# Negating the row maxima of two heads with one VectorE instruction in a graph attention kernel

## The reference: what is computed

```python
q, k, v = (proj(Wq, bq), proj(Wk, bk), proj(Wv, bv))
scores = jnp.einsum('bhqd,bhkd->bhqk', q, k) * SCALE
scores = scores * (adj_matrix + bond_matrix)[:, None, :, :]   # both are adj
attn = jax.nn.softmax(scores, axis=-1)
ctx = jnp.einsum('bhqk,bhkd->bhqd', attn, v)
out = jnp.einsum('bse,fe->bsf', ctx, Wo) + bo
return _layernorm(x + out)
```

## Time and profile before

| | us |
|---|---|
| median of 3 runs (437.01 to 439.08) | 437.6 |
| the profiled execution | 432.45 |
| its span in the trace | 430.8 |
| DVE busy | 387.9 (90%), 1592 instructions |
| PE busy | 383.4 (89%) |
| ACT busy | 360.5 (84%) |
| POOL busy | 249.6 (58%) |

### The profile page before, as it was taken

One profiled execution on the slowest core, in us unless ns is written; L12 is line 12 of the kernel. 1 busy time (PEld: TensorE's weight loads), 2 busy tenths in 40 slices (PEclk: granted clock), 3 DMA queues, 4 the chain that ended last, 5 costly groups with the idle time before them and its releaser, 6 DMA issues.

```text
span 430.8 us, 12136 instructions
## 1 busy us (share of the span) xinstructions
PE 383.4 (89%) x3628; PEld 291.0 (68%) x3628; DVE 387.9 (90%) x1592; ACT 360.5 (84%) x1223; POOL 249.6 (58%) x379
## 2 busy tenths in 40 slices
PE   8968999998989899998999999899898999997682
PEld 6755767776767676675777667677766767775452
DVE  4687999999999999999899999989999999999965
ACT  4588899888888888888988888899888789988760
POOL 3330656748385664748567474856747385554455
PEclk9999999999999999999999999999999999999998
DMA  8548869788887978878797888889788787978632
GB/s 288 168 107 217 235 165 304 175 265 217 232 242 181 303 159 252 247 202 263 192 295 182 243 242 210 254 203 294 178 251 228 163 256 178 276 170 214 155 90 73
DMA packets 58658, 92.28 MB, mean 214 GB/s; under 512 B 7777, under 2 KB 47970, under 8 KB 58594
## 3 DMA queue, kind: packets, MB, share of 16 engines
q1 hardware_dynamic: 45266, 66.35, 60.8%
q10 hardware_dynamic: 13328, 25.17, 16.9%
HBM read 26.22 MB, written 8.39 MB: 80 GB/s over the span
## 4 chain that ended last, share of the span: by engine, by line
ACT 31%; PE 20%; DVE 16%; SPq 12%; issue 11%; DMA 7%; POOL 1%; ACTq 0%; DVEq 0%; POOLq 0%
ACT probs L705 24%; SPq L202 8%; DVE probs L502 8%; PE ctx_bank L396 5%; DMA v_boxed<-v 5%; DVE boxes L520 5%; PE proj_bank L325 4%; PE out_bank L343 4%; SPq L211 4%; PE row_bank L256 3%; ACT turned_probs L713 3%; ACT inverse L719 2%; PE turn_bank L273 1%; ACT kq L733 1%; DVE top L502 1%
## 5 line engine op out<-in xcount | busy, mean ns | idle before, releaser
L705 ACT ACTIVATE probs<-probs,low_top 128x256 f32<-128x256 f32 x512 | 254.7, 504 | 41.5 <-DVE low_top L511 40.4
L502 DVE CUSTOM_DVE_ANT_0 probs<-row_bank,adj_rows 128x256 f32<-128x256 f32 x512 | 188.0, 416 | 5.1 <-PE row_bank L256 4.8
L520 DVE STREAM_TRANSPOSE boxes<-probs 128x1536 f32<-128x1536 f32 x62 | 109.7, 1769 | 1.0 <-DMA carried<-boxes 1.0
L705 ACT ACTIVATION_READ_ACCUMULATOR probs<-probs,low_top 128x1 f32 x512 | 99.3, 194 | 0.0
L325 PE MATMUL proj_bank<-xt_parts,w_parts 128*128 128x512 f32 x360 | 99.3, 411 | 0.0
L325 PEld LDWEIGHTS proj_bank<-xt_parts,w_parts 128*128 128x128 f32 x360 | 63.0, 188 | 30.2 <-issue 19.6
L256 PE MATMUL row_bank<-kq 32*128 32x256 f32 x1024 | 73.3, 400 | 5.2 <-DVE top L502 3.9
L396 PE MATMUL ctx_bank<-carried,v_boxed 128*32 128x256 f32 x744 | 59.5, 382 | 19.1 <-DMA v_boxed<-v 16.1
L842 POOL COPY wide<-shares 128x512 f32<-128x512 f32 x32 | 19.5, 610 | 74.9 <-DVE shares L528 74.9
L396 PEld LDWEIGHTS ctx_bank<-carried,v_boxed 128*32 128x32 f32 x744 | 31.2, 109 | 43.5 <-issue 30.7
L413 PE MATMUL out_bank<-w_parts,ctx_parts 128*128 128x256 f32 x372 | 51.5, 287 | 9.9 <-issue 6.7
(11 more groups left out here) (85 smaller groups left out, 467.2 us busy)
## 6 DMA issues: line engine op xcount, KB each, us to landing
carried<-boxes SPq DMA_DIRECT2D x248, 192.0 KB, 4.0
adj_rows<-in_adj ACTq DMA_DIRECT2D x16, 512.0 KB, 6.6
xr<-in_x ACTq DMA_DIRECT2D x16, 512.0 KB, 6.9
v_boxed<-v SPq DMA_DIRECT2D x124, 64.0 KB, 2.5
out<-result ACTq DMA_DIRECT2D x31, 256.0 KB, 4.8
xt<-in_x_t SPq DMA_DIRECT2D x15, 512.0 KB, 4.2
xt<-in_x_t SPq DMA_DIRECT2D x2, 256.0 KB, 3.2
w_whole<-in_wk ACTq DMA_DIRECT2D x2, 128.0 KB, 3.4
```

What stands on the lines that cost most here:

```text
L502: last = nc.vector.tensor_tensor_reduce(probs[:, h % RING, t * S:(t + 1) * S], row_bank[j][:, t * S:(t + 1) * S], adj_rows[:, (g // 2) % 2 ...
L520: nc.vector.transpose(boxes[:, n % 2].rearrange("p a h (f q) -> p (h f) a q", q=D), probs[:, first:first + BOXED, :].rearrange("p h (f a k ...
L705: last = nc.scalar.activation(tile, tile, ACT.Exp, bias=low_top[:, g % 2, J * c + j, t:t + 1], accum_out=sums[:, g % 2, t, j * T + c:j * T ...
```

## The change

`lower_top`, one head at a time, becomes `lower_tops`, two heads at a time. It reads 128x4 maxima instead of 128x2 and raises `top_ready` by 2. The first, for heads 0 and 1, stands behind the masking of the third head (j == 2); the second, for heads 2 and 3, at the end of the group. ACT still waits for `top_ready` of J * n + j + 1 before each head. Nothing else changes.

```diff
-            def lower_top(n, j):
-                g, place = n // T, J * (n % T) + j
-                dve.wait_ge(rows_used, J * n + j + 1)
-                nc.vector.tensor_reduce(low_top[:, g % 2, place, :], top[:, g % 2, place, :].unsqueeze(2), AXIS.X, ALU.max,
-                                        negate=True).then_inc(top_ready, 1)
+            def lower_tops(n, half_):
+
+                g, place = n // T, J * (n % T) + 2 * half_
+                dve.wait_ge(rows_used, J * n + 2 * half_ + 2)
+                nc.vector.tensor_reduce(low_top[:, g % 2, place:place + 2, :], top[:, g % 2, place:place + 2, :].unsqueeze(3),
+                                        AXIS.X, ALU.max, negate=True).then_inc(top_ready, 2)
...
                 for j in range(J):
                     reduce_rows(n, j)
-                    if j > 0:
-                        lower_top(n, j - 1)
-                lower_top(n, J - 1)
+                    if j == 2:
+                        lower_tops(n, 0)
+                lower_tops(n, 1)
```

## The result

| | before | changed |
|---|---|---|
| median, us | 436.89 (435.11 to 439.08, 6 runs) | 450.01 (446.82 to 453.18, 6 runs) |
| ratio to before | 1 | 1.030 (95% interval 1.023 to 1.036) |
| span of the profiled execution, us | 430.8 | 451.2 |
| DVE busy, us | 387.9 | 383.7 |
| ACT busy, us | 360.5 | 360.0 |

The profiled execution of the changed kernel took 452.88 us, near the upper end of its six (their spans lie between 445.2 and 451.5). The profiled execution before took 432.45 us, less than each of the six in the table. So the two profiles lie 20.4 us apart and the medians 13.1, and the medians are the measure of the change. The forecast was 450.6 for the median.

What follows compares the result with a forecast made beforehand. Bound: ACT's work plus DVE's stretch between two graphs. Loops add 12.4 us; with start, end and remainder +13.0, taking the profiled execution from 432.45 to about 445.5; the median, 5.15 above, becomes 450.6 (range 448.0 to 456.5).

Steps and rivals of the forecast that it cites:

- The loop as the bound, 12.20 us: Once per graph, ACT's eight heads plus DVE's stretch from reciprocal to first negation set the pace: 12.20 us without other waits.
- 0.69 us per graph: Between reciprocal and first exponential: the third head's masking delays the first negation, lengthening the loop from 12.20 to 12.89 us.
- Negations that go give back 0.07 to 0.22 us per group, 6.4 us in all, none of it on the path: Two of four negations per group go: DVE saves 0.10 us in each of 64 groups, without shortening the loop.
- 19 us of busy time "without use": DVE's recorded busy time over the whole run should fall by 128 x 0.15 = 19 us without use.
- The rule on grouping against the trace: On DVE's negations: the skill's overhead rule alone gave 7.7 us gained; the trace's 40.4 us of ACT waiting spoke against.
- What the longer loop hides: ACT's projection waits of 0.77 and 1.00 us vanish, both below 1.38, so already longer loops gain less than 0.69 us.
- the stall of 1.08 us: A stall on ACT with no other engine as its releaser, expected to stay and counted in the sum.
- The end gives 0.69 back: In the last graph ACT waits 1.49 us for PE, whose work hangs on DVE's, so 0.69 us returns.
- The wait at the reciprocal, 39 us: DVE's wait for ACT at the reciprocal should grow from 20.1 to about 39 us, in all graphs.
- Nothing is hidden: Rival: PE's waits stay on top, all 31 loops pay 0.69 us, 459 us; hidden in part or not at all, 0.22.
- no difference: Rival: transfers and PE's projection set the pace in every graph, 0.69 us vanishes in slack, 437 to 439 us; chance 0.03.
- DVE is the bound: Rival: DVE's own work sets the pace, so removed negations count in full, 6.4 us, time 431; chance 0.03.

## Why the prediction was right, step by step

- **The loop as the bound, 12.20 us.** Right. It is closed by both sides' waits in the traces, and cutting it turned the change's 3% loss into a gain of 1 to 2%.
- **0.69 us per graph.** Right: quiet loops 12.89 to 12.93 after. The distance from reciprocal to first exponential, the quiet loop and the median go up together: 1.69 to 1.72 us, 12.20 and 437 to 438; 1.88, 12.40 and 442.17; 2.38 to 2.41, 12.90 and 449.4 to 450.0; 3.07 to 3.10, 13.59 and 469.69.
- **Negations that go give back 0.07 to 0.22 us per group, 6.4 us in all, none of it on the path.** The second half held; the size was wrong, and so was its sign. Between maskings one negation still costs 0.07 us (228.05 to 228.12), so one of 0.07 is saved. At the end the one merged negation costs 0.32 us where the two single ones cost 0.22; the prediction had put one alone at 0.07 to 0.22. A group costs DVE 0.39 us (0.07 + 0.32) where it was 0.36 (0.07 + 0.07 + 0.22): nothing is saved at all. It is tempting to say that the first of two single ones filled the time until the fourth head's maxima had landed. The kernel with head 0 negated at once has a single negation with nothing in between:

```profile
207.24 0.08 DVE L502 DVE_READ_ACCUMULATOR2_ANT top<- 128x1 f32 x1
207.36 0.15 DVE L511 TENSOR_REDUCE low_top<-top 128x2 f32<-128x2 f32 x1
...
207.48 0.42 DVE L502 CUSTOM_DVE_ANT_0 probs<-row_bank,adj_rows 128x256 f32<-128x256 f32 x1
```

It costs 0.24 us and starts 0.12 after the accumulator read; the merged one starts 0.19 after it (228.80 to 228.99). And the kernel with both pairs at the end, where a merged negation stands in front of the last one, takes 0.32 us as well (248.68 to 249.00). So nearly all of the difference goes with the merged form and not with what stands ahead of it; why it starts later is open. The forecast did not feel the wrong size, since that work was off the path. For the same reason the 19 us of busy time "without use" were wrong: busy time fell by 4.2 us (387.9 to 383.7), because negations and maskings overlap in the records.
- **The rule on grouping against the trace.** The Trainium skill (Perfetto Trace Analysis, Optimizing Scalar/DVE Operations) says that grouping can improve throughput if the engine is saturated. The estimate of 7.7 us gained, by that rule alone, is out: VectorE was not saturated at this place, since it waited at 30 of 32 reciprocals (24.6 us), and the cost of its negations didn't shrink.
- **What the longer loop hides.** Right in some executions, not in the profiled one. With the same delay of head 0 ACT waited for PE's projection 1.1 us in all in the kernel with late single negations, and 2.5 in the one with the change in first groups. In the profiled execution of the changed kernel it was 5.9 us, all but 0.73 of them after graph 0, up to 1.52 us at a time, though I had computed that waits up to 1.38 us vanish. The worst place begins with a wait for a transfer:

```profile
186.15 1.35 PE L396 MATMUL ctx_bank<-carried,v_boxed 128*32 128x256 f32 x18 [2.67 <-DMA v_boxed<-v]
...
187.64 0.70 PE L396 MATMUL ctx_bank<-carried,v_boxed 128*32 128x256 f32 x2
```

and, in a view of busy time by stretch (stretch, its length, busy us of PE, PEld, DVE, ACT and POOL, then the granted clock, DMA share and GB/s), the clock behind it:

```profile
183.60:186.10 2.50, 0.00 (x0) 0.00 (x0) 1.96 (x12) 1.08 (x4) 1.56 (x3) 1.00 0.69 153
187.20:189.50 2.30, 2.30 (x24) 1.31 (x13) 0.81 (x3) 1.40 (x6) 0.00 (x0) 0.50 0.96 218
...
316.17:318.96 2.79, 0.00 (x1) 0.03 (x1) 2.12 (x12) 1.21 (x5) 1.72 (x3) 1.00 0.53 138
319.00:323.00 4.00, 4.00 (x52) 3.10 (x56) 3.07 (x10) 3.56 (x14) 1.90 (x3) 1.00 0.95 239
```

PE stood idle for 2.67 us; a microsecond later the granted clock was 0.50, the 1.2 GHz level, and a pair of matmuls took 0.70 us where it took 0.39 at full clock. That loop took 15.89 us, the longest. The clock fell once more among the loops of this trace, behind an idle stretch of 2.23 us before 131.46 (0.50 from 133.00 to 136.00, in the loop of 14.87 us), but it stayed at 1.00 behind the longest one, 2.79 us before 318.96 (the last two rows, in the loop of 14.42 us). So late transfers alone can make a loop long, and the half clock came on top in two cases; its share of the time wasn't measured. My sum had priced PE's chain from one undisturbed trace. Six loops, five with a wait of ACT for the projection and one in which DVE's box transpose waited 1.28 us for a transfer, hold 8.4 us above 12.905 each (the sum of 13.49, 14.87, 15.89, 13.57, 14.42 and 13.56 less six times 12.905), which, less the stall of 1.08 us that I had kept on ACT and that did not come back, is the distance of 7.3 between the forecast span of 443.9 (445.5 less 1.65) and the measured 451.2. The faster executions, with a mean clock of 0.994, have spans of 445.2 and 445.3.

The same sum says how much was hidden. The full delay is 21.4 us (31 times 0.69). The medians rose by 13.1, so 8.3 were hidden, as the forecast had it (13.0). The profiled spans rose by 20.4, so only 1.0 was hidden there: in place of the 9.0 us of waits above the quiet loops before there were 8.4 after. For the median the forecast added 5.15 us, the distance of the median from the profiled execution before. After the change the profiled execution lay 2.9 us above the median instead. The two errors, 7.4 us too little for the profiled execution and 8.0 too much between it and the median, cancel to 0.6. That is luck for the number; what stands is the rise between the medians.
- **The end gives 0.69 back.** Right: from graph 31's first exponential to the end it was 27.6 us (403.21 to 430.8), and is 27.0 (424.21 to 451.2), 0.6 less.
- **The wait at the reciprocal, 39 us.** It was 24.6. No DVE time was saved, and part of its slack turned up elsewhere: the wait for `out_bank` ahead of `add_residual` is 8.5 us in 24 graphs, where it was 1.6 in 2. It grows with the delay, to 35.0 us in the kernel with both pairs at the end. PE's `project_out` waits for ACT's `copy_v`, which is 0.69 us later; that this is the cause was not tested.
- **The rivals.** "Nothing is hidden" (459 for the median) and "no difference" did not happen. "DVE is the bound" did not either, and a reciprocal without a wait (graphs 14 and 30 before) is no sign of it by itself. TensorE's clock isn't the cause of the loss either: in the kernel before, executions with a mean clock of 0.992 to 0.997 have spans of 430.8 to 438.3, and the changed one has 445.2 and 445.3 at 0.994.

## What to carry to other kernels

When two engines wait for each other once per iteration, neither's busy share counts, only the stretch of each that lies between the two waits; an instruction count that falls by half elsewhere is worth nothing against one more tile inside that stretch. Before merging small operations, look at who waits for the first of them, and measure the merged one from start to start where it will stand: it can cost more than the two that it replaces. A cure that worked here is to move what closes the loop (the reciprocal, 1 to 2%) behind what the other engine waits for.

## What the runs showed of the hardware

A short VectorE instruction between longer ones cost 0.07 us of its engine's time at a recorded 0.15. Directly behind the result it reads a single one (128x2) cost 0.24 us and a merged one (128x4) 0.32, more than two single ones in that place (0.22). And in one execution idle stretches of PE of 2.23 and 2.67 us were followed by stretches at half clock, in which a pair of matmuls took 0.70 us instead of 0.39, while one of 2.79 us was not.
